# Layer 1 of a two-layer model: one loop over sequences becomes an attention pass and an expert pass

## What is computed

```
xn = layernorm(x)
# gated linear attention, 4 heads, chunks along the sequence
q, k, v, g = xn@Wq, xn@Wk, xn@Wv, xn@Wg;  gk = log_sigmoid(xn@gk_w1@gk_w2 + b)/16
r1 = x + (gated, normed GLA output) @ Wo
# softmax attention, 16 heads of 8 channels, then four experts
q, k, v = xn@Wq2 + bq, xn@Wk2 + bk, xn@Wv2 + bv
attn    = softmax(q k^T / sqrt(8)) v              # 512 x 512 scores a head
xf      = layernorm(xn + attn@Wo2 + bo)
e(token) = floor(xf . router_w + router_b) mod 4
ff      = sum_e [e(token)==e] * (relu(xf@W1[e] + b1[e]) @ W2[e] + b2[e])   # all four are computed
out     = r1 + layernorm(xf + ff)
```

## Time and profile before

| what | value |
|---|---|
| time, median of 2 runs (3894.93 to 3898.93) | 3896.93 us |
| span of the profiled execution, first to last instruction | 3872.1 us |
| what the median has beside that span | 24.8 us |
| PE / DVE / ACT / POOL busy | 80% / 51% / 36% / 12% of the span |
| layer 1's first load of x | at 1397.6 us |
| round of layer 1 (14 between 1498.4 and 3639.1 us) | 152.9 us |

### The profile page before, as it was taken

One profiled execution on the slowest core, in us unless ns is written; L12 is line 12 of the kernel. 1 busy time (PEld: TensorE's weight loads), 2 busy tenths in 40 slices (PEclk: granted clock), 3 DMA queues, 4 the chain that ended last, 5 costly groups with the idle time before them and its releaser, 6 DMA issues.

```text
span 3872.1 us, 47514 instructions
## 1 busy us (share of the span) xinstructions
PE 3095.8 (80%) x16292; PEld 2116.7 (55%) x16292; DVE 1983.7 (51%) x3726; ACT 1399.3 (36%) x2025; POOL 448.2 (12%) x619
## 2 busy tenths in 40 slices
PE   5998899989899947778777787787687777877887
PEld 4777777777777733434444444445344444443454
DVE  4655656655666535544535535445355354454452
ACT  2333333323333324253252451442533523524424
POOL 0011000010000110020120111110201201101111
PEclk9999999999999967777786786777777867767778
DMA  2000000000000020110110100100101101011000
GB/s 71 6 6 5 11 5 5 5 5 10 6 5 5 5 69 16 18 33 10 24 34 7 27 24 17 27 18 17 33 7 27 34 7 27 18 18 33 18 17 7
DMA packets 61948, 71.40 MB, mean 18 GB/s; under 512 B 5564, under 2 KB 39376, under 8 KB 60880
## 3 DMA queue, kind: packets, MB, share of 16 engines
q1 hardware_dynamic: 61912, 70.93, 7.3%
HBM read 44.63 MB, written 26.21 MB: 18 GB/s over the span
## 4 chain that ended last, share of the span: by engine, by line
PE 30%; DVE 12%; issue 6%; DMA 6%; ACT 5%; SPq 3%; POOL 2%; ACTq 0%; DVEq 0%; POOLq 0%
DVE b_row_max L1383 7%; PE b_psum L1161 7%; DMA b_k_stack<-qk_scratch 4%; PE b_psum L1108 4%; PE b_psum L1073 3%; PE b_psum L962 3%; SPq L917 3%; ACT b_prob L1239 3%; PE b_psum L1096 2%; PE b_psum L964 2%; PE b_psum L963 2%; PE b_psum L1041 1%; PE b_psum L1025 1%; DMA b_x<-x_scratch 1%; DVE b_acc L1465 1%
## 5 line engine op out<-in xcount | busy, mean ns | idle before, releaser
L1383 DVE TENSOR_REDUCE b_row_max<-b_psum 128x2 f32<-128x1024 f32 x512 | 592.3, 1218 | 145.3 <-PE b_psum L1073 144.8
L1239 ACT ACTIVATE b_prob<-b_psum 128x1024 f32<-128x1024 f32 x512 | 494.0, 1034 | 173.0 <-PE b_psum L1096 172.8
L1073 PE MATMUL b_psum<-b_k_stack,b_q_stack 24*128 24x512 f32 x1024 | 293.8, 719 | 259.8 <-DMA b_k_stack<-qk_scratch 143.8
L1260 ACT ACTIVATE b_hid<-b_psum,b_cols 128x512 f32<-128x512 f32 x256 | 176.0, 687 | 726.5 <-PE b_psum L964 726.4
L1073 PEld LDWEIGHTS b_psum<-b_k_stack,b_q_stack 24*128 24x128 f32 x1024 | 111.7, 259 | 439.5 <-DVE b_row_max L1383 267.2
L1108 PE MATMUL b_psum<-b_prob,b_v_aug 128*32 128x512 f32 x2048 | 320.2, 702 | 11.2 <-ACT b_prob L1239 10.9
L1096 PE MATMUL b_psum<-b_q_stack,b_k_stack 26*128 26x512 f32 x1024 | 216.4, 565 | 123.3 <-ACT b_prob L1239 80.0
L1161 PEld LDWEIGHTS b_psum<-b_w_plain,b_hid 128*128 128x128 f32 x2048 | 294.8, 229 | 19.5 <-ACT b_hid L1260 10.7
L1161 PE MATMUL b_psum<-b_w_plain,b_hid 128*128 128x128 f32 x2048 | 291.7, 311 | 5.9 <-ACT b_hid L1260 5.9
L1096 PEld LDWEIGHTS b_psum<-b_q_stack,b_k_stack 26*128 26x128 f32 x1024 | 86.3, 205 | 261.8 <-ACT b_prob L1239 186.3
L528 DVE SCALAR_TENSOR_TENSOR a_kv_sb<-a_psum,a_bias,a_v_sb 128x512 f32<-128x512 f32 x128 | 96.0, 750 | 221.9 <-ACT a_v_sb L446 221.9
(11 more groups left out here) (242 smaller groups left out, 5804.3 us busy)
## 6 DMA issues: line engine op xcount, KB each, us to landing
b_q_stack<-qk_scratch SPq DMA_DIRECT2D x192, 64.0 KB
b_k_stack<-qk_scratch SPq DMA_DIRECT2D x192, 64.0 KB
qk_scratch<-b_qk_hi SPq DMA_DIRECT2D x16, 512.0 KB, 2.8
qk_scratch<-b_qk_lo SPq DMA_DIRECT2D x16, 512.0 KB, 3.7
a_xin<-in_x SPq DMA_DIRECT2D x17, 256.0 KB, 2.9
a_raw<-in_a_split SPq DMA_DIRECT2D x4, 1024.0 KB, 6.1
x_scratch<-a_x SPq DMA_DIRECT2D x16, 256.0 KB, 2.4
b_x<-x_scratch SPq DMA_DIRECT2D x16, 256.0 KB, 2.8
```

Source lines behind the costliest of these rows:

```text
L1073: mm = nc.tensor.matmul(psum[:, 2 + 2 * (i % 2) + x, :], q_stack[r, j, cut(t)], k_stack[r, j, :], start=True, stop=True)
L1239: nc.scalar.activation(prob[:, p % 4, :, :], psum[:, 2 + 2 * (p % 2):4 + 2 * (p % 2), :], ACT.Exp, scale=DH1 ** -0.5).then_inc(S["exp"], 1)
L1260: nc.scalar.activation(hid[:, i // HID % 2, i % HID, :], bank(f"w1{i}"), ACT.Relu, bias=col("b1", i)).then_inc(S["hid"], 1)
L1383: nc.vector.tensor_reduce(row_max[:, t, at:at + HPG + 1:HPG], psum[:, 2 + 2 * (i % 2):4 + 2 * (i % 2), :], AX.X, ALU.max).then_inc(S["row_ ...
```

## The change

Layer 1 becomes two functions, `attention` and `experts`, and each runs over all sixteen sequences.

`attention` has rounds of 32 slots. A slot p holds the score pair p of one sequence (stage C, round r), the maximum pair p of the next one (stage B, r+1), every second slot a `pv`, and other steps at fixed slots: the front of r+2 (A0), the gated linear attention of r+1 (A1), the maxima's last turn (B2) of r, and the tail of r-1 (C2). Scores have banks 2 and 3 and maxima banks 4 and 5, one pair of banks each and no second buffer. Scores read `cq`, `ck`, maxima `bq`, `bk`. Only one row of the maximum is kept (25 rows instead of 26), and it goes from SBUF to SBUF. The stacks are now laid out in DRAM by the stores: 24 stores of 32 partitions (`stack_scratch`), then loads of 24 partitions, eight for each half of B and of C. `h_blk` is one POOL instruction instead of 12. xn + bias, r1 and xf go by way of DRAM. Rounds -2 to 1 and 14 to 16 are written out, with the steps whose sequence exists.

`experts` loads xf and r1 and walks 16 `w1` and 4 `y` a sequence with nothing of the attention between; `y` alternates between banks 0 and 1, the rest use six banks in turn, and the norm of the sequence before and the router of the next one are laid between.

The weights are split in four pieces instead of two, and 16 small DMAs load the biases in the new order of channels.

```diff
+    put(0, "B2", "mT", 1)
+    put(0, "A1", "gz")
+    put(1, "C2", "pv", STEPS - 1)
+    put(2, "C", "Cld", 1)
+    put(2, "B", "Bld", 1)
+    put(3, "A1", "vg", 0)
+    put(4, "A1", "gz2")
+    put(4, "C2", "aoT", HPG - 1)
+    put(5, "A1", "vg", 2)
+    put(7, "A1", "eexp")
+    put(8, "C2", "mwo")
+    put(9, "A1", "gqk")
+    put(10, "C2", "norm1")
+    put(11, "A1", "mv")
+    put(12, "A0", "front")
+    put(13, "A1", "U")
+    put(14, "A0", "front2")
+    put(14, "A1", "A", 0)
+    put(16, "A1", "A", 2)
+    put(17, "B", "mT", 0)
+    put(18, "A0", "mqk")
+    put(18, "B", "Cld", 0)
+    put(19, "A0", "mqklo")
+    put(19, "A1", "O", 0)
+    put(20, "A0", "qk_st")
+    put(21, "A1", "O", 1)
+    put(21, "A0", "Bld", 0)
+    put(22, "A1", "O2")
+    put(24, "A1", "O3")
+    put(29, "A1", "gwo")
...
+    for p in range(PAIRS):
+        order += [("C", "score", p), ("B", "max", p)]
+        if p >= 3 and p % 2:
+            order.append(("C", "pv", (p - 3) // 2))
+        if p % 8 == 2 and p > 8:
+            order.append(("C", "ao", p // 8 - 1))
+        if p % 8 == 4 and p > 8:
+            order.append(("C", "aoT", p // 8 - 1))
+        order += at[p]
...
+        PV, SCORE, MAX, RING = 0, 2, 4, (1, 6, 7)
...
+                    elif kind == "qk_st":
+                        until("qk_lo", stage, 2, 2)
+                        for w, parts in enumerate(((qk_hi, qk_hi, qk_lo), (qk_hi, qk_lo, qk_hi))):
+                            if w:
+                                until("max_filled", stage, PAIRS, -STEPS)
+                            for g in reversed(range(ROWG)):
+                                for c, src in enumerate(parts):
+                                    sp.dma_start(stacked(stage, w, 32 * g + DH1 * c, DH1).rearrange("d j s -> (d j) s"),
+                                                 src[32 * g:32 * g + 32, w, :].bitcast(F32)).then_inc(S["qk_st"], 16)
+                    elif kind == "Bld":
+                        if i == 0:
+                            until("qk_st", stage, 384, 384)
+                        else:
+                            until("max_filled", stage, PAIRS, 0)
...
                     elif kind == "max":
+                        if i % STEPS == 0:
+                            until(f"b_in{i // STEPS}", stage, 128, 128)
+                        until("row_max", stage, PAIRS, i)
...
                     elif kind == "score":
+                        if i % STEPS == 0:
+                            until(f"c_in{i // STEPS}", stage, 128, 128)
+                            until(f"m_in{i // STEPS}", stage, 32, 32)
+                        until("exp", stage, PAIRS, i)
...
+def experts_order():
+    for e in range(EXPERTS):
+        for m in range(HID):
+            order.append(("D", "w1", HID * e + m))
+            if m == 1 and e:
+                order.append(("D", "y", e - 1))
...
+        Y, RING = (0, 1), (2, 3, 4, 5, 6, 7)
```

More of the change, by code:

```diff
@@ L647, in layer1, with experts_uses, attention @@
+def experts_uses(step):
+    _, kind, i = step
+    if kind == "w1":
+        return [f"w1{i}"]
+    return {"hT": ["hT"], "maskT": ["maskT"], "b2": ["b2"]}.get(kind, [])
+def attention(nc, psum, w_hi, w_lo, w_plain, col, qk_bias, ident, causal, bo_row, rows, minus_half, eps,
+              d_x1, d_stack, d_xnb, d_r1, d_xf):
     with ExitStack() as ctx:
         def sb(name, shape, dt=F32):
[L649 to L652 removed]
@@ L792, in layer1 @@
-        AHEAD = {"front", "xT", "gz", "vg", "gqk", "mqk", "kT", "U", "A", "O", "oT", "gwo", "mv", "max", "mT"}
-        front = [("xT", 0), ("gz", 0), ("vg", 0), ("vg", 2), ("gqk", 0), ("mqk", 0), ("kT", 0), ("U", 0), ("A", 0), ("A", 2),
-                 ("O", 0)]
-        MAXES = 2 * STEPS
-        round_order = [("front", 0)]
[L797 to L801, removed]
-            if i % HPG == 1 and i > 1:
-                round_order.append(("aoT", i // HPG - 1))
-            if 2 <= i < 2 + len(front):
-                round_order.append(front[i - 2])
@@ L932, in _, with rounds, until @@
             run(sp, rounds)
-            sp.wait_ge(S["out_out"], 16 * BATCH)
+            sp.wait_ge(S["r1_out"], 16 * BATCH)
+            sp.wait_ge(S["xf_out"], 16 * BATCH)
         @block.tensor
         def _(pe):
-            def rounds(b, order):
-                n = b + 1
-                here, before = ring_list(order), ring_list(round_order)
+            def rounds(base, add, now):
+                looped = not isinstance(base, int)
+                def until(name, stage, per, k, back=0):
+                    hold(pe, S[name], base, per, (add - back + OUT_OF[stage]) * per + k)
@@ L941, in take @@
                 def take(u, known=""):
[L943 to L954 removed]
+                    here = [x for step in now for x in attention_uses(step)]
@@ L955, in take @@
+                    here = here[:here.index(u)]
+                    for back in range(3):
+                        if back:
+                            if not looped and add - back < -2:
+                                return
+                            here = [x for step in (order if looped else live(add - back)) for x in attention_uses(step)]
+                        same = [x for x in here if bank_of[x] == bank_of[u]]
                         if same:
                             s, per, k = FREE[same[-1]]
-                            pe.wait_ge(S[s], b * per + k if kind else b * per)
+                            if s != known or back:
+                                until(s, stage_of[same[-1]], per, k, back)
+                            return
```

1249 lines of the change are left out of this document (720 added, 529 removed), and 6 rows, old and new, of the table FREE.

## The result

The changed kernel takes **3706.86 us** (median of two runs, 3688.82 and 3724.91) against 3896.93: ratio 0.9511 [0.94, 0.9621]. That is 190 us less; forecast were 337 less. Four more runs, beside runs of the kernel before of 3885.31, gave 3737.95 and a ratio of 0.9625 [0.9598, 0.9652].

A forecast was written before the change was run, and what follows sets the result against it. No engine was taken to bound the whole round: DMA waits, PE in scores, low-clock PE alternating with DVE. Terms: 1397.6 + 6 + 1661 (attention) + 2 + 471 (experts) = 3538; with 24.8, 3562, taken as 3560 us; range 3330 to 3770.

The forecast's parts named there:

- rival 3: Attention rounds: waits between engines that the slot sum misses, 8 to 10 us a round, 3700 us in all; chance 8%.
- Start: Before layer 1's first load: 6 us more, for 16 small DMAs at 0.34 and two more weight pieces.
- Rounds: Attention loop: fourteen rounds at 98 us, 1372 us, between 85 at the high clock and 118 at the low.
- Ends of the attention pass: Rounds outside the fourteen: 32 us for round -2, 87 for -1, 92 for 14, 63 for 15, 15 for 16.
- Experts: Expert pass: 28 us a sequence, 448 for sixteen, plus 12 at the start and 11 at the end: 471 us.
- Which clock? ... I take the same.: Attention pass: PE keeps layer 1's earlier clock, 0.76 (high level 52% of the time), giving 98 us a round.
- The slots: Attention: DVE's loop 1.83 or 2.13 us; PE with pv 1.67 or 3.02, without 0.67 or 1.16 (high/low clock).
- The gain's origin: Per sequence, 98 + 29 for 152.9 us: mainly expert matmuls freed from maxima, plus two DMA waits of about 17.
- Number 1: Rival on attention: the clock stays high, 85 us a round and 23 less at the ends, 3340 us; chance 12%.
- Number 2: Rival on attention: the clock stays low, 118 us a round, 3879 us, no change; chance 9%.
- Number 4: Rival on attention: stacks come late at slot 0, +34 us in fifteen rounds at half pace, 4070 us; chance 5%.
- The chain of slot 20: Attention: stack stores, then B's first half, 28.4 us at the earlier pace, against slots 20 to 31; nothing charged.

The follow-up runs named there:

- Experiments 9 and 10: The edit of number 1 plus two zero-product matmuls behind the maximum pair in eleven even slots, on 128 rows (9) or 24 (10): 3456.1 and 3465.67 us.
- experiment 4: Changed kernel with the maximum's reduction reading only the first 256 of 512 keys in each bank: 3598.48 us, ratio 0.9171.
- Experiment 5: Kernel before the change, with all 32 maxima and mT put ahead of hT and the experts: 3941.54 us, ratio 1.0146.
- edit of number 1: Changed kernel with each slot's maximum pair on the two row groups that the score pair does not use: 3505.58 us, ratio 0.9026.
- number 11: Changed kernel with maxima on the other row groups, PE's own steps in even slots, and 128-row zero-product matmuls in eleven even slots: 3549.99 us, ratio 0.9118.
- number 6: Changed kernel with nearly all of PE's other steps moved from slots with a pv to even slots: 3623.7 us, ratio 0.9323.
- number 7: Changed kernel with PE's other steps moved to even slots and the maximum pair on the other row groups: 3462.67 us, ratio 0.8908.

## Why the prediction was right, and where it was off

The direction and the shape held; the time lies inside the range but 147 us over the forecast. It is outside the forecast's own range of 3450 to 3670, as the round of 106.8 is outside 98 give or take 7. What caught it is the part of the range that was added for rival 3, and that rival's mechanism didn't occur: so much was luck. Term by term, from the forecast's 3538 to the span of 3687:

- **Start:** first load at 1416.0 where 1403.6 were forecast: +12.4. The sixteen small DMAs and the weight pieces were priced at their issue alone. What else the 12 us hold wasn't taken apart; in the other profiled execution of the same kernel the load starts at 1409.8.
- **Rounds:** 106.8 for 98: fourteen times 8.8 = +123.
- **Ends of the attention pass:** 1805.9 us in all (1416.0 to 3221.9) for 1663, less the 123 above: +20. Around the loop the clock was low too, 0.55 to 0.57 from 1454 to 1660 us.
- **Experts:** 465.1 for 471: -6. The 27.5 us a sequence at a clock of 1.00 bear out the 28 read from one sequence.
- **Around the span:** the forecast added 24.8. The profiled execution of the changed kernel has 1.8 between span and time; the 24.8 was the difference between one execution and the median of others. This error was a gain of 23, and the median's 18 above the profiled execution made up for most of it.

**The step that failed was "Which clock? ... I take the same."** The clock of the attention pass was 0.67 instead of 0.76. The sum of slots and fillers up to that step stood within 3 us a round. The formula with its ends of 85 and 118 gives, at 0.67 (the high level for 34% of the time), s = 0.42 and 104 us. The single rounds say much the same without the formula: on their line a clock of 0.76 gives 102.5 - 4 x 0.79 = 99.3, against the 98 forecast. So of the 8.8 us that a round is over, the clock holds 6.2 by the formula and 7.5 by the rounds, 87 to 105 us over fourteen rounds, and the size of slots and fillers the other 1.3 to 2.6.

Why was it wrong to take 0.76 over? That was a mean over stretches of 0.92 and of 0.66. The new slots are no mean of these: every second one has PE waiting for an exponential. The stretch with the same pattern, a short pair and then a wait for another engine, was that of the maxima, and its clock was 0.66. That likeness is an argument and not a test. Experiments 9 and 10 show that filling PE's waits raises the clock.

**The slots** were right. With pv, 3.02 forecast and 3.02 in the timeline; without, PE's share 1.16 and 1.15. The bounds for a pair behind a pair on the same rows were 0 and 0.73; it is 0.56, and the score pair ahead of it takes 0.60 rather than 0.73, so the errors cancel. That 0 was to be had on other rows the forecast wrote down as a bound and didn't follow up; it was the best edit here. The slot without pv was charged to DVE's loop (2.13); it took 1.99, with ACT as the last releaser, and experiment 4, with 3 to 5.5 of 17 us, confirms that the lost double buffer bounds few slots. (DVE's loop at the low clock adds up to 2.11 and not 2.13.)

**The gain's origin** was weighed wrongly: the prediction said "mainly" that experts no longer take turns with maxima, and about 17 us for two DMA waits. A sequence went from 152.9 to 134.3 us, 18.6 less. Experiment 5 shows that experts apart from maxima give nothing alone (1.0146). And the waits for DMAs of the kernel before, over 15 or 16 sequences, are nearly as large as the gain:

```profile
PE b_psum L1073 <- DMA b_k_stack<-qk_scratch: 143.8, 15, 14.1
...
DVE b_stats L1282 <- DMA b_x<-x_scratch: 101.7, 16, 6.9
```

That is 9.6 and 6.4 us a sequence, and neither wait is in the new loop. So, as a balance and not as a test: the hidden loads are worth some 16 us, and what the experts won (27.5 us for a stretch of 72.9, 45.4 less) was nearly all given back, since maxima beside scores at a clock of 0.67 take 106.8 us where the scores had 56.5 and the work before them 6.3, 44.0 more. No run hides the loads alone, so how the gain divides isn't shown.

**Rivals.** Number 1 (clock high, 3340) fell: 0.67. (Its "23 less at the ends" should read 38, 289 less 251; its sum has the right terms.) It was also what the prediction drew from Part 1 of the page "TensorE: Matmul & The Clock Gate" of the Trainium skill, and the measurement decides against that reading. Its premise was wrong besides: a round does have one idle time of microseconds, the 4.05 us of PE in slot 1, and behind it the clock went from 1.00 (until 2299.68) to 0.50 (from 2303.02). The Trainium skill's section "A second HAM failure mode: psum-queue depth-cycling" on that page tells of short idle times of PE between groups of matmuls that make the clock go back and forth. This loop looks like it: slots wait 0.77 and 0.94 us, and the granted clock of a round lies between the levels, with stretches at each. Number 2 (clock low, 118 a round) is what single rounds came near to, 115.1 and 116.3 at a clock of 0.56; a whole loop never did (110.7 at most). Number 3 (missed waits, 3700) gave about the measured time by another mechanism; its waits aren't there to that size, since at the clock of 0.76 only 1.3 to 2.6 us a round are missing. Number 4 (late stacks) didn't occur: PE waits for no DMA, in a loop that moves 59 GB/s. The chain of slot 20 was shorter than the 28.4 us taken: in the timeline of SP's queue the stores start at 2360.08 and the last load of B's first half is issued by 2376.66, 16.6 us. The gate of slot 0 and the step of slot 21 make long slots, as said (2295.07 to 2300.85, 5.78 us, and 2362.75 to 2370.92, 8.2 us).

**Still open:** what sets the clock. The edit of number 1 takes busy time from PE and raised it from 0.67 to 0.77. Nor is the busy share a guide: the changed kernel has 89% at 0.68 (94.36 of 105.80) and number 9 has 87% at 0.85. Two neighbouring stretches of one round of the changed kernel say the same:

```profile
2363.14:2393.20 30.06, 28.34 (x110) 12.78 (x107) 13.74 (x14) 11.75 (x14) 5.26 (x2) 0.50 0.27 68
2349.78:2363.14 13.36, 12.12 (x86) 7.29 (x85) 9.60 (x12) 8.52 (x12) 0.72 (x1) 0.99 0.33 92
```

The first starts behind a wait of 0.83 us, holds 94% of PE work and runs at the low level for 30 us; the one before it holds 91% and runs at the high one. So idle time is a part of the answer (numbers 9 and 10) and not all of it.

## What to carry to other kernels

When a change moves work into a new mixture, read the clock of the old stretch whose pattern of work and waits resembles the new one, not the mean of the stage; here the clock alone was 87 to 105 of the 147 us missed. That such a stretch foretells the clock fits this one case and wasn't tested on another. When two streams of small matmuls share slots, put them on different row groups before anything else (12.4 of 106.8 us a round for two changed indices), and fill PE's idle slots with its own steps, but nothing that another engine waits for. Before crediting a reordering with a gain, add up the waits that it also hides. Cutting the loop at a load that comes once a round gives a dozen repeats of the same work at different clocks, and so the price of the clock from one execution.

## What was unexpected of the hardware

- Adding 22 useless matmuls to a round made it shorter, 92.1 us for 94.35, with the clock at 0.85 for 0.77; the same matmuls in a kernel whose slots were fuller (number 11) made it 6.8 us longer.
- Pairs of 24- and 25-row matmuls start 0.01 us apart on different row groups and 0.60 apart on the same ones at the low clock.
- The granted clock has patterns of its own in a loop of equal rounds: alternating 0.63 and 0.69 in number 6; in the first execution of the changed kernel 0.56, 0.64 and 0.67 and then a steady 0.68 with one round at 0.72, and 0.56 to 0.72 in no order in another. Its six executions spread over 1.7% (3688.8 to 3751.0), while the four of number 7 lie within 1 us.
- PE can be busy for 94% of 30 us and be held at the low level all the while.
